# The four corners of a bilinear sample summed by one strided reduction on VectorE

## The reference, cut to what matters

```python
x = L0(x)   # self-attention with 32 reduced channels, softmax over 1024 pixels, residual
x = L1(x)   # 1x1 conv to 32 channels, deformable 3x3 conv, 1x1 conv back, residual, relu
x = L2(x)   # self-attention with 16 query/key channels, softmax over 1024 pixels, residual
x = L3(x)   # group norm, self-attention with 128 channels, residual
```

```python
h = relu(bn(conv1x1(x, w1)))                       # (4, 32, 32, 32)
off = conv3x3(h, woff) + boff                      # 27 planes: 9 y, 9 x, 9 mask
samp = (gather(y0, x0)     * (wy0 * wx0) + gather(y0, x0 + 1)     * (wy0 * wx1)
      + gather(y0 + 1, x0) * (wy1 * wx0) + gather(y0 + 1, x0 + 1) * (wy1 * wx1))
samp = samp * sigmoid(mask)
out = einsum('bckhw,ock->bohw', samp, w2) + b2     # then bn, relu, conv1x1, bn, + x, relu
```

## Time and profile before

| | |
|---|---|
| median of 3 runs | 571.77 us (570.62 to 573.72) |
| the profiled execution: its time, its span | 573.63 us, 571.6 us |
| busy: PE, DVE, ACT, POOL | 491.7 (86%), 316.8 (55%), 288.4 (50%), 293.3 (51%) us |
| mean granted clock of TensorE | 0.91 |

### The profile page before, as it was taken

The page is one execution under the profiler, slowest core; times in us unless marked ns, Lnnn a source line. Parts: engine busy times, 40 slices in busy tenths (PEclk is TensorE's granted clock), DMA queues, the critical chain, the costliest instruction groups (busy, mean ns, idle before and its releaser), DMA issues.

```text
span 571.6 us, 7362 instructions
## 1 busy us (share of the span) xinstructions
PE 491.7 (86%) x2688; PEld 328.6 (57%) x2688; DVE 316.8 (55%) x558; ACT 288.4 (50%) x485; POOL 293.3 (51%) x292
## 2 busy tenths in 40 slices
PE   5897897869889778889998969998957999896996
PEld 3443633525435346856686845776844677693775
DVE  4746225476556766766678556558565525624321
ACT  4275461374177655245575434584532557442652
POOL 0000177777777777777777777777777300000000
PEclk9999778659879879979999979999987899997999
DMA  5000111112212111211313111112111100100000
GB/s 218 0 1 1 46 56 50 56 47 58 86 46 94 46 52 48 55 47 46 94 47 92 52 46 52 50 54 87 52 52 46 28 1 1 38 1 0 1 1 37
DMA packets 12562, 26.92 MB, mean 47 GB/s; under 512 B 4976, under 2 KB 5616, under 8 KB 12528
## 3 DMA queue, kind: packets, MB, share of 16 engines
q0 software_dynamic: 9216, 18.89, 11.7%
q1 hardware_dynamic: 2880, 6.52, 3.0%
q10 hardware_dynamic: 432, 1.05, 0.5%
HBM read 21.99 MB, written 4.46 MB: 46 GB/s over the span
## 4 chain that ended last, share of the span: by engine, by line
POOL 49%; PE 26%; issue 15%; DVE 3%; ACT 3%; DMA 2%; POOLq 0%; DVEq 0%; ACTq 0%
POOL got L298 49%; PE pd L604 5%; PE pq L596 2%; PE pc L586 2%; PE pa L586 2%; PE pq L363 2%; PE pa L334 2%; DMA xall<-x_dram 1%; PE pa L541 1%; PE pc L541 1%; DVE neg_max L1601 1%; PE pc L388 1%; PE pc L334 1%; PE pa L570 1%; PE pd L328 1%
## 5 line engine op out<-in xcount | busy, mean ns | idle before, releaser
L298 POOL DMA_INDIRECT got<-cell_table,rows_all x288 | 293.1, 1018 | 155.4 <-issue 87.5
L1601 DVE TENSOR_REDUCE neg_max<-pa 128x1 f32<-128x1024 f32 x48 | 58.7, 1223 | 39.7 <-PE pa L334 39.3
L604 PEld LDWEIGHTS pd<-v3T,probsT 128*128 128x128 f32 x512 | 60.3, 192 | 11.1 <-ACT probsT L1112 8.5
L604 PE MATMUL pd<-v3T,probsT 128*128 128x128 f32 x512 | 63.3, 277 | 3.2 <-ACT probsT L1112 2.4
L363 PE MATMUL pq<-q_stack,k_stack 128*128 128x512 f32 x120 | 55.1, 516 | 9.5 <-ACT expT L1141 5.1
L334 PE MATMUL pa<-k_stack,q_stack 96*128 96x512 f32 x96 | 40.2, 505 | 10.5 <-DVE neg_max L1601 7.3
L1141 ACT ACTIVATE expT<-pq 128x512 f32<-128x512 f32 x64 | 35.6, 595 | 23.9 <-PE pq L363 23.0
L363 PEld LDWEIGHTS pq<-q_stack,k_stack 128*128 128x128 f32 x120 | 24.6, 217 | 36.2 <-ACT expT L1141 11.9
L1678 DVE TENSOR_TENSOR weighed<-got,corner_w 128x1152 f32<-128x1152 f32 x32 | 43.3, 1354 | 3.2 <-DMA got<-cell_table,rows_all 2.1
L1112 ACT ACTIVATE probsT<-pq 128x1024 f32<-128x1024 f32 x32 | 32.7, 1022 | 15.0 <-PE pq L596 10.3
L1225 ACT ACTIVATE expT<-pq 128x512 f32<-128x512 f32 x56 | 31.1, 598 | 15.4 <-PE pq L363 14.3
(11 more groups left out here) (173 smaller groups left out, 788.6 us busy)
## 6 DMA issues: line engine op xcount, KB each, us to landing
got<-cell_table,rows_all POOLq DMA_INDIRECT x288, 2.5
cell_table<-tabS SPq DMA_DIRECT2D x4, 512.0 KB, 2.6
out_dram<-cells SPq DMA_DIRECT2D x8, 256.0 KB, 2.1
xall<-x_dram SPq DMA_DIRECT2D x2, 512.0 KB, 8.6
wts<-weights_dram SPq DMA_DIRECT2D x1, 778.5 KB, 6.1
xall<-x_dram ACTq DMA_DIRECT2D x2, 256.0 KB, 5.2
xall<-x_dram ACTq DMA_DIRECT2D x1, 512.0 KB, 8.4
cell_table<-tabS SPq DMA_DIRECT2D x4, 64.0 KB, 2.7
```

Source lines behind the costliest of these rows:

```text
L298: nc.gpsimd.indirect_dma_start(got[:, t, k, :], None, tables[b % 2], bass.IndirectOffsetOnAxis(ap=rows_all[:, b, at:at + 1], axis=0)).then ...
L604: last = nc.tensor.matmul(d0[:, 0:C], probsT[:, tile(j)], v3T[:, j, :], start=j == 0, stop=j == TILES - 1)
L1601: nc.vector.tensor_reduce(neg_max[:, t:t + 1], pair[:, :], axis=X, op=ALU.max, negate=True)\
```

## The change

The two additions and the drain between them become one reduction over a rearranged view of the same buffer. Its innermost dimension is the corner, so it reads element r of the four corners, which lie 32 numbers (128 bytes) apart, then element r + 1, and so on. The wait ahead of it, the semaphore behind it and the last drain stay, and so do all lists of calls.

```diff
             def l1_add(b, t):
                 if TILES * b + t >= 2:
                     dve.wait_ge(st_mm, TILES * b + t - 1)
-                nc.vector.tensor_tensor(weighed[:, :, 0:2 * R], weighed[:, :, 0:2 * R], weighed[:, :, 2 * R:4 * R], ALU.add)
-                dve.drain()
-                nc.vector.tensor_tensor(samples[:, t % 2, :].rearrange("p (k r) -> p k r", r=R), weighed[:, :, 0:R],
-                                        weighed[:, :, R:2 * R], ALU.add).then_inc(sample_ready, 1)
+                nc.vector.tensor_reduce(samples[:, t % 2, :].rearrange("p (k r) -> p k r", r=R),
+                                        weighed[:, :, :].rearrange("p k (c r) -> p k r c", r=R), axis=X, op=ALU.add)\
+                    .then_inc(sample_ready, 1)
                 dve.drain()
```

## The result

The changed kernel takes 577.77 us (median of 11 runs, 575.37 to 580.56) against 572.12 us for the kernel before on the same chip (11 runs). The ratio is 1.0091, with a 95% interval of 1.0067 to 1.0115: slower by 0.7% to 1.2%, clear of noise. Forecast was 579.0 us, in a range of 569 to 589 us. The profiled execution has a span of 576.4 us, against 571.6 before.

The account below looks back on a forecast made before the run. Gathers and the other engines' attention work were taken as parallel chains, attention alone bounding after 439.14 us. Ten exposed turns, less the 2.15 us gather wait, gave 6.75 us, plus 0.4: 571.8 + 7.2 = 579.0 us, range 569 to 589.

Parts of the forecast that it names:

- The price of the stepped read: VectorE's new reduction, reading at a step of 32 numbers, takes 2.28 us, 1.0 us more than the two additions.
- The upper end: VectorE's reduction pays twice the 0.8 ns a number: 3.2 us, 1.9 us more than the two additions.
- Ten turns exposed, 22 covered: VectorE's delay reaches the end in ten turns, +6.75 us after subtracting 2.15 us; idle time hides it in 22.
- the surcharge: Extra time of VectorE's reduction over the two additions because its read is stepped: 1.0 us a turn.
- the 0.4 us for leaks: Added for the 22 turns where idle time hides VectorE's delay, some with only tenths in hand: +0.4 us.
- GpSimd: Gathers no longer contend with two-input additions: some 4 us less busy time, worth 2.15 us at most.
- the wait of 2.15 us: VectorE's only wait for a gather, ahead of the multiplication of turn (3, 6) at 439.14 us; predicted to go.
- The clock: TensorE's half-clock stretches after stalls, 1.7 us each: put at zero, with 1.7 us either way in the range.
- The first: Rival: VectorE's stepped read costs nothing, reduction 1.36 us, gather wait goes; 569.7 or 568.0 us; chance 0.31.
- The second: Rival: VectorE's stepped read costs far more, 3.2 us a reduction, +1.9 us a turn; 590 us; chance 0.13.
- The third: Rival: VectorE's reduction takes about 2.3 us but the delay is covered nearly everywhere; 572.1 us; chance 0.07.

Follow-up runs that it names:

- The measurement of steps: Two profile-only kernels: each turn's sum in the changed kernel became a reduction at another step or group size; groups of four from step 4 to 288 took 2.13 to 2.23 us.
- The two split kernels: Reduction only in the ten turns called exposed, or only in the 22 others, two additions elsewhere: 579.0 us (1.0116) and 569.97 us (0.9945) against the kernel before.
- the ten-turn kernel: Reduction only in the ten turns called exposed, the kernel before's two additions in the other 22: 579.0 us, ratio 1.0116 to the kernel before.
- the kernel with two inputs: Changed kernel with one 1152-number addition of the multiplied buffer to itself in place of the reduction, samples left at zero: 575.33 us, ratio 1.0075 to the kernel before.
- the contiguous one: Changed kernel with the reduction adding four neighbouring numbers (step 1) instead of corners 32 apart: 567.66 us, ratio 0.9928 to the kernel before.
- the 22 turns: Reduction only in the 22 turns called covered, the kernel before's two additions in the ten others: 569.97 us, ratio 0.9945 to the kernel before.

## Why the prediction was right, step by step

**The price of the stepped read.** Predicted 2.28 us from the 0.8 ns a number of line 1672, measured 2.18. The choice of the nearest row decided the case, and it decided rightly. Part of that was luck. The price was known only for a write of 72 numbers at a step of 4, and nothing in the trace said that a read pays the same. The measurement of steps shows the same size, 0.72 ns, for reads of groups of four and more at steps of 4 and more; for groups of two or three, or at steps of 2 and 3, the same row would have forecast a cost that is not there. The upper end, which had the price grow with the step, is excluded: 288 costs what 4 costs.

**Ten turns exposed, 22 covered.** The two split kernels confirm it as a division. By place, TensorE's idle time against the kernel before, of which two waits stand in no row so far:

```profile
193.12 0.68 PE L402 MATMUL pc<-wts,probs 128*128 128x129 f32 x4 [0.56 <-issue]
...
420.53 0.66 PE L550 MATMUL pq<-wts,oT 128*128 128x128 f32 x4 [0.18 <-DVE oT L1720]
```

| turn | predicted | measured, from the rows |
|---|---|---|
| (1, 0) | +0.8 | +0.7: at line 402, 1.29 for 0.56 us; the wait at 409 itself did not grow |
| (1, 2) | +1.0 | +0.9: 1.82 for 0.92 |
| (1, 3) | +0.7 | +0.5: 0.48 for none |
| (2, 3), (2, 4) | +1.5 | +1.2: 2.25 for 1.01 |
| (3, 1) | +1.0 | +1.0: 1.19 for 0.22 |
| (3, 4) | +0.9 | +0.9: 1.08 for 0.18 |
| (3, 5), (3, 6) | +2.0 - 2.15 | -0.35: 2.75 for 3.10 |
| (3, 7) | +1.0 | +0.9: 1.46 for 0.59 |
| sum | +6.75 | +5.75 |

At line 402 the profile names no releaser. In both traces it starts 0.1 us after VectorE's `l0_add` (line 1638) ends, at 193.01 us before and 192.25 us after, so it is VectorE that it waits for, one call earlier than the prediction had it.

One of the ten was right for a wrong reason. The transposes at 419.42 us belong to turn (3, 3), not to (3, 4): TensorE's list has `l1_turn(3, 3)` ahead of the two groups of line 550 and `l1_turn(3, 4)` far behind them, and in the changed kernel they start at 425.50 us, before the sum of (3, 4) ends at 426.26. The delay reaches TensorE all the same, through the normalized tiles that VectorE computes next (lines 1718 and 1720) and that the wait above is for.

With the 0.89 us that a turn really lost (2.18 - 1.29) in place of 1.0 in the same walk, the sum is 7.8 - 2.15 = 5.6 us. The timed loss is 5.65 us by medians and 5.2 us by the ratio (3.8 to 6.6 by its interval). So the term that was too large is the surcharge, by a tenth, and the 0.4 us for leaks were not seen.

**GpSimd.** The direction was right and the size too small: 6.6 us less busy time, not 4. The estimate also rested on a misread row: only the gather at 118.20 us ran beside an addition, while the one at 119.58 ran beside the multiplication of the next turn, which the change keeps. The 30 gathers that began beside an addition took 5.7 us more than the median in all, which is most of the 6.6 us. Here the relief was worth nothing of its own: as the ten-turn kernel shows, VectorE's delay alone is enough to take the wait of 2.15 us away. That the relief is real is shown by the kernel with two inputs, and that it pays when VectorE keeps pace by the contiguous one and by the 22 turns. The Trainium skill's sentence (SBUF — State Buffer, Who interferes with whom) that a two-input Vector instruction contends with a GpSimd instruction that reads SBUF, and a `tensor_reduce` not, agrees with all of these.

**The clock.** I had put it at zero, with 1.7 us either way. Both things happened: a new stretch behind turn (1, 2), 1.75 us, and a shorter one behind turn (3, 6), where the four matmuls took 2.64 instead of 3.62 us. The span grew by 4.8 us, less than the 5.75 us of idle time, so in this pair of executions the gains at the clock seem to outweigh the losses by about a microsecond; this is a difference of two sums, not a measurement. Part of the gain has nothing to do with the change: from 155 to 170 us the clock was 0.69 in this profile of the kernel before and 1.00 in its second one.

**The rivals.** The first is what the contiguous read does, 568 us, and only the step keeps it from being true here. The second is excluded by the 2.18 us and by the measured steps; its price was also added up wrongly, since the ten turns at +1.9 us give 18 us and not 16, and the time 592 us. The third would have left TensorE's waits as they were. They grew in every place named but two: at (1, 0) the wait just ahead of it took the growth, and at (3, 6) the gather's wait that went outweighed it.

## What to carry to other kernels

Count the numbers that an instruction reads, and look at how they lie: one instruction for two is no gain on VectorE when it reads 1152 numbers instead of writing 864, and a read that goes round four places, 4 or more numbers apart, took 1.6 times as long as one along memory (2.18 against 1.35 us). Then ask of each place where the instruction stands what comes next on its engine: the same 0.9 us cost 0.5 to 1.0 us each in ten places and less than nothing in 22. And where gathers bound the kernel, look at what VectorE runs when each one begins: here two instructions of the same length differed by 1.5% of the kernel's time because one had two inputs and the other one.

## What the runs showed of the hardware that was not expected

- Reductions in pairs are free of the surcharge at steps of 4 to 288 (0.75 to 0.77 us for 576 numbers), in threes nearly so (1.14 us for 864 against 1.04 at step 2), and from four on it is whole at steps of 4 and more (2.09 to 2.23 us for 1152). At steps 2 and 3 groups of four are free. The Trainium skill (Vector Engine (DVE) Microarchitecture Reference, section 5.2 Measured stream behaviour on trn2) has both ends, 1.73 ns a column for a source that hops at every element and the full rate for a read that alternates between two regions, but it asks for runs of two adjacent words for the full rate, which the free steps of 2 and 3 words don't have: these runs decide.
- A two-input addition of 1.36 us made GpSimd's 288 gathers take 297.3 us, a one-input reduction of 1.35 us 286.5 us. A gather that begins while such a two-input instruction runs ends, with few exceptions, 0.8 us after that instruction; one that begins beside the reduction takes its usual 0.94 us.
- A stall of TensorE that grew from 0.92 to 1.82 us had a stretch at the lower clock behind it in two executions out of two, and in three other kernels with the same stall, and cost more through it (1.75 us) than by itself (0.9 us).
